# Paired causal attentions: the sums over four blocks of keys, spread over four steps or taken in one visit

## The reference

```
q, k, v = split heads of (x @ W + b)            # 16 heads of 8
att = einsum('bhqd,bhkd->bhqk', q, k) / sqrt(8) (+ bias)
att = softmax(where(causal, att, -inf))
y   = einsum('bhqk,bhkd->bhqd', att, v)
x   = layernorm(x + y @ W_proj + b_proj)
```

## Time and profile before

| what | us |
|---|---|
| median of 3 runs | 2263.75 |
| runs from, to | 2261.84, 2269.63 |
| profiled execution, device time | 2265.27 |
| its span in the profile | 2263.3 |
| first stage, from its first `turned` to its last `group` | 162.3 |
| fifth stage (L2 attention), the same | 151.8 |

### The profile page before, as it was taken

How to read it: one execution, slowest core, us unless ns; L and a number is a source line. 1 busy time by engine, 2 the same in 40 slices (tenths; PEclk the granted TensorE clock), 3 DMA queues, 4 the chain that set the end, 5 groups by cost and what they waited for, 6 DMA issues and landing times.

```text
span 2263.3 us, 44486 instructions
## 1 busy us (share of the span) xinstructions
PE 1973.9 (87%) x17496; PEld 1179.8 (52%) x17496; DVE 1460.6 (65%) x2920; ACT 1171.9 (52%) x1950; POOL 813.2 (36%) x1153
## 2 busy tenths in 40 slices
PE   5886689998878989998999788999899898999888
PEld 2342466666644544554665344444555665666446
DVE  5775687878768777773555776121677676767464
ACT  2575356656622444555333467322576675757432
POOL 4544343433126748343001331000545344453033
PEclk7998799999989999999999899999999999999999
DMA  4430111111234434210201220000465564655152
GB/s 130 140 103 2 25 31 28 30 33 26 63 107 127 125 98 137 59 49 1 104 1 50 88 91 20 32 0 1 154 206 175 173 208 131 207 174 168 51 114 56
DMA packets 183990, 199.10 MB, mean 88 GB/s; under 512 B 55922, under 2 KB 152486, under 8 KB 179302
## 3 DMA queue, kind: packets, MB, share of 16 engines
q1 hardware_dynamic: 183782, 196.27, 29.5%
HBM read 93.53 MB, written 92.08 MB: 82 GB/s over the span
## 4 chain that ended last, share of the span: by engine, by line
PE 34%; DVE 6%; ACT 6%; issue 3%; DMA 2%; POOL 2%; SPq 1%; DVEq 0%; ACTq 0%; POOLq 0%
PE PS L2104 5%; PE PS L357 4%; PE PS L2351 3%; PE PS L2367 3%; PE PS L1957 3%; PE PS L2339 3%; ACT AR L2509 2%; PE PS L1944 2%; PE PS L1947 2%; PE PS L2703 1%; PE PS L604 1%; PE PS L2691 1%; PE PS L2693 1%; DMA AR<-ZD 1%; PE PS L583 1%
## 5 line engine op out<-in xcount | busy, mean ns | idle before, releaser
L1282 ACT ACTIVATE AR<-PS 128x1024 f32<-128x1024 f32 x160 | 162.6, 1024 | 123.9 <-PE PS L1031 123.0
L725 ACT ACTIVATE AR<-PS 128x1024 f32<-128x1024 f32 x160 | 162.9, 1024 | 93.3 <-PE PS L583 48.0
L1135 DVE TENSOR_REDUCE AR<-PS 128x2 f32<-128x768 f32 (+1 forms) x192 | 159.9, 864 | 55.8 <-PE PS L1011 30.7
L2565 POOL TENSOR_TENSOR RA<-AR,RA 128x288 f32<-128x288 f32 x128 | 88.2, 698 | 275.4 <-DVE RA L2441 142.2
L2509 ACT ACTIVATE AR<-PS,AR 128x512 f32<-128x512 f32 x256 | 174.0, 687 | 24.2 <-DVE AR L2430 24.0
L2430 DVE TENSOR_REDUCE AR<-PS 128x2 f32<-128x1024 f32 x128 | 156.8, 1225 | 12.9
L2339 PE MATMUL PS<-AR 64*128 64x200 f32 (+2 forms) x1280 | 147.0, 354 | 2.9 <-ACT AR L2509 2.9
L1828 POOL TENSOR_TENSOR AR<-AR 128x1024 f32<-128x1024 f32 x32 | 75.4, 2358 | 174.4 <-DVE AR L1676 174.4
L2351 PEld LDWEIGHTS PS<-CC,AR 64*128 64x128 f32 x2048 | 77.8, 140 | 98.1 <-issue 76.7
L2351 PE MATMUL PS<-CC,AR 64*128 64x64 f32 x2048 | 92.3, 229 | 38.7 <-DVE AR L2436 11.7
L2339 PEld LDWEIGHTS PS<-AR 64*128 64x128 f32 x1280 | 111.3, 193 | 6.3 <-ACT AR L2509 3.2
(11 more groups left out here) (366 smaller groups left out, 4984.4 us busy)
## 6 DMA issues: line engine op xcount, KB each, us to landing
ZD<-RC SPq DMA_DIRECT2D x32, 1152.0 KB
AR<-ZD SPq DMA_DIRECT2D x32, 640.0 KB
ZP<-AR SPq DMA_DIRECT2D x128, 160.0 KB, 2.7
SP<-AR SPq DMA_DIRECT2D x40, 384.0 KB, 2.6
AR<-SP SPq DMA_DIRECT2D x128, 96.0 KB
RA<-SP SPq DMA_DIRECT2D x32, 384.0 KB
SP<-AR SPq DMA_DIRECT2D x40, 256.0 KB, 2.9
RC<-RC SPq DMA_DIRECT2D x64, 130.0 KB
```

The costliest lines, as they stand in the source:

```text
L725: e.activation(self.PT[m % 6], C.PS[:, 2 * s:2 * s + 2, :], ACT.Exp).then_inc(S["s_turned"].sem, 1)
L1135: i = e.tensor_reduce(nm[:, :, 4 * up + q:4 * up + q + 1], src[:, :, a:a + wd], AX, ALU.max, negate=True)
L1282: e.activation(self.PT[m % 6], C.PS[:, 2 * s:2 * s + 2, :], ACT.Exp).then_inc(S["s_turned"].sem, 1)
```

## The change

The four `group` steps of a group, which stood at g = 4 of the group itself and at g = 0, 1, 2 of the next, now stand together at g = 1 of the next group. Their order (kb = 0, 1, 3, 2), their matmuls and the columns they cover stay. The `take` stays at g = 2. There are seven buffers of turned probabilities in place of six, and the indices and the wait before the exponential follow.

```diff
+        self.PT.append(cv(128, 2, 512))
...
-            if m >= 5 and m % 5 < 3:
-                plan.append(("group", k - 1, (1, 3, 2)[m % 5]))
-                if m % 5 == 2:
+            if m >= 5 and m % 5 == 1:
+                plan.extend(("group", k - 1, kb) for kb in (0, 1, 3, 2))
+            if m >= 5 and m % 5 == 2:
                     plan.append(("take", k - 1))
...
-            if 0 <= m < N and m % 5 == 4:
-                plan.append(("group", k, 0))
...
-                             self.PT[at % 6][:, r, a:a + wd], start=kb == 0, stop=kb == 2)
+                             self.PT[at % 7][:, r, a:a + wd], start=kb == 0, stop=kb == 2)
...
-            k, g = (m - 6) // 5, (m - 6) % 5
+            k, g = (m - 7) // 5, (m - 7) % 5
             w.wait_ge(S["t_group"], k, (0, 0, 3, 3, 2)[g])
             w.wait_ge(S["t_turned"], m)
-            e.activation(self.PT[m % 6], C.PS[:, 2 * s:2 * s + 2, :], ACT.Exp).then_inc(S["s_turned"].sem, 1)
+            e.activation(self.PT[m % 7], C.PS[:, 2 * s:2 * s + 2, :], ACT.Exp).then_inc(S["s_turned"].sem, 1)
```

More of the change, by code:

```diff
@@ L784, in on_gpsimd @@
             m, = key
-            P, g = self.PT[m % 6], m % 5
+            P, g = self.PT[m % 7], m % 5
             own = P[:, :, 0:128] if g < 2 else P[:, :, 0:256] if g < 4 else P.rearrange("a r (p j) -> a (r p) j", p=2)[:, :, 0:128]
```

## The result

| | before | after |
|---|---|---|
| median of 4 runs each, us | 2266.69 | 2295.70 |
| from, to | 2261.84, 2270.01 | 2291.86, 2299.42 |
| profiled execution, device time | 2265.27 | 2296.53 |
| first stage, first `turned` to last `group` | 162.3 | 174.4 |
| fifth stage, the same | 151.8 | 165.0 |

The changed kernel is 1.0134 times as slow [1.0111, 1.0157], 29 us, where 9 were forecast: the sign was right and the size three times too small, outside the range. Two later comparisons gave 26 and 25 us. The two stages make 25 of the 31 us between the profiled executions; the rest lies before, between and behind them. Most of it is likely spread between executions: outside the two stages the program takes 1949.2 us before and 1955.2 in this profile, but 1950.3 and 1951.9 in two later profiles of the changed kernel.

A forecast was written before the change was run, and what follows sets the result against it. PE was taken as the bound, with little room, slot waits deciding inside a group. The group terms summed to +9.5 on the profiled 2265.27, 2274.8; with the median 1.5 lower, 2273 us was predicted, range 2257 to 2284.

The forecast's parts named there:

- 0 and 1: Groups 0 and 1, both stages: bound by the first transfers, and the first visit falls out of them; -1.0 us.
- 13 to 15: Groups 13 to 15: few or no `scores`, ACT busy; last visit waits for the last exponential but can begin early; +0.8 us.
- The saving: PE's four visits a group, 2.72 us, become one of 2.28; 0.44 less a group, 14.1 us less PE work.
- The ordinary group: Group with two pieces: 0.44 saved, 1.3 more waited for slots; +0.87 us, or +0.71 to +0.78 in the fifth stage.
- Groups 2 to 4: Chain from `lin` through split, stores and fetch to `turned`: `lin` comes 1.8 us later, all follows; +3.6 for two stages.
- Group 8: ACT's table change for the layer norm: long visit lies there; 1.26 shorter plus 1.5 for slow matmuls, twice: -5.4 us.
- Group 12: Second sequence's layer norm starts at step 3 of group 11, its covering visits gone; +1.7 and +1.5, together +3.2 us.
- The recurrence part: Group 12's waits worked out step by step from slot hand-overs between PE, ACT and DVE: +1.7 and +1.5 us.
- The clock: TensorE's low clock in the sum: only group 8's slow matmuls, taken as another 1.5 us gained in each stage.
- Rival 3: Much slower: PE stands at layer norms of groups 11 and 15 bring low clock, 8 us more, 2281; chance 0.15.
- Rival 1: PE's saving arrives: readers have more slack than counted, the 14.1 us come off; 2250, down to 2244; chance 0.15.
- Rival 2: It cancels: slot waits come, but the 13.4 us of `ZM` waits go nearly altogether; about 2264; chance 0.30.

The follow-up runs named there:

- first kernel with fillings: Changed kernel plus 12, 12, 10 and 4 overwritten matmuls in the four stands for `ZM`, against the kernel before: +24.9 us, 1.0114.
- runs with half readers: Either kernel with ACT's exponentials and DVE's largest values in the two stages on half the columns: 2252.3 us (kernel before) and 2253.8 (changed).
- three fillings of 0.66 us: Changed kernel with matmuls filling the four `ZM` stands and 3 more ahead of each group's step 3 `turned`, against the kernel before: +19.9 us, 1.0090.

## Why the prediction was wrong in size

The terms of its sum, from the starts of the groups in the two profiles, both stages added:

| groups | forecast | measured |
|---|---|---|
| 5, 6, 7, 9, 10, 11 | +8.3 | +16.9 |
| 2 to 4 | +3.6 | +8.8 |
| 0 and 1 | -1.0 | -1.1 |
| 8 | -5.4 | -5.0 |
| 12 | +3.2 | +7.2 |
| 13 to 15 | +0.8 | -1.4 |
| sum | +9.5 | +25.4 |

- *The saving, 0.147 a visit and 14.1 us in all.* Right in size (2.29) and in not arriving.
- *The ordinary group.* Right in kind; +0.87 was forecast where the clock is high and +1.10 came in group 10, with +0.87 and +0.97 for 0.7 to 0.8 in the fifth stage (8.82 and 8.91, from 7.95 and 7.94). That makes some 2.5 us over the twelve groups, and 1.2 are the waits for `ZM`, which stayed. The other 5 are groups such as 9 (8.24 before, 11.22 after), whose visit ran at 1.2 GHz (143.32 above).
- *Groups 2 to 4.* That the whole chain from `lin` to `turned` moves was right. The 0.78, 2.28 and 0.6 ahead of `lin` were taken at full clock, and in this stretch three of the six visits took 3.50 to 3.96.
- *Group 8.* Right: 12.44 and 12.23 before, 10.12 and 9.51 after. Removing the visit from the stand at the table change gave what was forecast.
- *Group 12.* The recurrence part was right: in the fifth stage, in the first kernel with fillings, the visit of this group runs at full clock and the group lasts 11.56, +1.8 where +1.5 was forecast. In the changed kernel it lasts 13.25 and the visit 4.05. In the first stage the low clock had come in group 11 already, behind waits of 0.75, 0.72 and 0.53: the `turned` at 172.30 is slow before the wait of 1.70.
- *The clock.* This is the step that failed. The sum held "another 1.5 for the slow matmuls" in group 8 as the clock's only term, a gain. Rival 3 had the mechanism, but made it a matter of two layer norms and of stands of 3.20. Low clock came behind a stand of 1.35 (group 5 above) and in places behind waits of 0.75 and less, in 13 of the 16 groups of the first stage and 7 of the fifth, where it had been in 7 and 2. The two stages have 34 us more of it, which at 0.34 each is an estimated 12 us of time that the sum put at nothing. Rival 3's 8 us for four places was the right order for what the prediction had as unlikely.
- *Rival 1* (the saving arrives) fell by the runs with half readers: even there nothing arrives. *Rival 2* (the `ZM` waits vanish) fell too: 13.2 us of them are left in 6 places, of 13.4 in 7, and without them the difference is the same. The 1.2 us that the sum took off for them was not seen.

With the estimated 12 us for the clock the sum would have been +21.5, against +25.4. The rest is in the ordinary groups (0.1 to 0.2 each) and the waits for `ZM`.

## What to carry to other kernels

Merging short instructions of a busy engine pays only if its neighbours have work meanwhile. Count what is issued to them between two hand-overs, and place the merged piece right behind the instruction that feeds the scarcest reader: one step made 17.7 us here. (That was tried at one pair of steps, 1 and 2, with 24 and with 32 matmuls.) Then price the clock: if a change adds stands to TensorE, take the slow pace for a share of the work after them, above all for the piece that was made long.

## What was not expected of the hardware

- TensorE's time at 1.2 GHz differs by 40 us between runs of one kernel (199 to 241), and it goes with the time of the run (correlation 0.86): 0.34 us each. So much of what looks like noise between runs goes with the clock; which of the two brings the other is not shown.
- A stand of 1.35 us was followed by 3.4 us at 1.2 GHz; four matmuls put into it, which left 0.38 of it, took that away and made the group 1.65 us shorter.
- A visit of 32 matmuls that lasts 2.36 at full clock lasted up to 4.28 with the low one.
- Seven in place of six buffers, 4 KB a partition more, changed nothing that 10 runs could tell.
- Extra matmuls in front of a wait cost nothing where the wait covers them: group 10 of the changed kernel lasts 8.66 with and without the three fillings of 0.66 us.
